# Two preactivated 3x3 convolutions on one Trainium2 core: from 64x64 quarters in two halves to 32x32 blocks in four streams

## What is computed

```python
# x: (8, 16, 512, 512) fp32
def _gn(v, G=8, eps=1e-5):            # group norm over 2 channels x 512 x 512, no weights
    ...
# layer 0: the 3x3 kernel of each image comes from spectral weights, turned by an angle
#          that depends on batch statistics of a 1x1 projection of gn(x)
x = x + _L0_conv_ref(_gn(x), w_fft_real, w_fft_imag, rot_w, rot_b, bn_gamma, bn_beta)
# layer 1: a plain 3x3 convolution with circular padding (written with FFTs)
x = x + _L1_conv_ref(_gn(x), weight)
```

## Time and profile before

| What | us |
|---|---|
| time, median of 2 runs | 1798.58 (1798.43 to 1798.72) |
| profiled execution, time | 1799.18 |
| its span, first to last instruction | 1797.4 |
| PE busy in the span | 1655.8 (92%), 29275 matmuls |
| PE weight loads (PEld) busy | 1246.7 (69%) |
| VectorE busy | 1388.3 (77%) |
| ScalarE busy | 1172.3 (65%) |
| POOL busy | 128.1 (7%) |
| mean DMA rate | 229 GB/s |
| mean granted TensorE clock | 0.977 |

### The profile page before, as it was taken

How to read it: one execution, slowest core, us unless ns; L and a number is a source line. 1 busy time by engine, 2 the same in 40 slices (tenths; PEclk the granted TensorE clock), 3 DMA queues, 4 the chain that set the end, 5 groups by cost and what they waited for, 6 DMA issues and landing times.

```text
span 1797.4 us, 65352 instructions
## 1 busy us (share of the span) xinstructions
PE 1655.8 (92%) x29275; PEld 1246.7 (69%) x29275; DVE 1388.3 (77%) x2175; ACT 1172.3 (65%) x1044; POOL 128.1 (7%) x361
## 2 busy tenths in 40 slices
PE   5887888487779999999999999999999999999899
PEld 5787888333356667887688668866786678666655
DVE  6989999779878787877887888787888788787500
ACT  6888888468556666666666666666666666666444
POOL 0000000120110010002000200020002001100100
PEclk9999999789899999999999999999999999999999
DMA  9999999355446665656666666566656665665245
GB/s 386 421 422 422 422 422 422 146 156 152 126 138 212 206 193 192 218 190 197 207 207 203 188 211 211 198 191 214 202 193 198 206 207 192 202 206 193 96 193 201
DMA packets 101782, 411.56 MB, mean 229 GB/s; under 512 B 16883, under 2 KB 19496, under 8 KB 85160
## 3 DMA queue, kind: packets, MB, share of 16 engines
q1 hardware_dynamic: 100744, 407.81, 64.6%
q0 software_dynamic: 800, 0.15, 0.1%
HBM read 271.82 MB, written 136.07 MB: 227 GB/s over the span
## 4 chain that ended last, share of the span: by engine, by line
PE 72%; DVE 14%; issue 5%; DMA 5%; POOL 1%; ACT 1%; SPq 1%; DVEq 0%; POOLq 0%; ACTq 0%
PE ps L406 36%; PE ps L399 34%; DVE x L635 7%; DMA x<-x_pix 5%; DVE nat L684 2%; DVE x L848 2%; DVE stats L886 1%; ACT x L475 1%; PE ps L350 0%; PE ps L351 0%; SPq L248 0%; PE ps L358 0%; POOL sm L606 0%; DVE ps L854 0%; PE ps L354 0%
## 5 line engine op out<-in xcount | busy, mean ns | idle before, releaser
L399 PE MATMUL ps<-nat,wc 64*64 64x512 f16 (+1 forms) x12480 | 1269.1, 379 | 45.7 <-DVE nat L684 16.5
L406 PE MATMUL ps<-x,wc 64*64 64x512 f16 (+2 forms) x12585 | 1256.4, 375 | 15.3 <-POOL x L615 14.8
L399 PEld LDWEIGHTS ps<-nat,wc 64*64 64x64 f16 x12480 | 721.8, 107 | 252.6 <-issue 38.2
L406 PEld LDWEIGHTS ps<-x,wc 64*64 64x64 f16 x12585 | 732.2, 107 | 193.4 <-POOL x L615 18.5
L500 ACT ACTIVATE nat<-xin,gnp 128x1024 f16<-128x1024 f32 (+1 forms) x264 | 299.9, 1137 | 318.6 <-PE ps L399 306.1
L848 DVE SCALAR_TENSOR_TENSOR x<-ps,gnp,x 128x1024 f16<-128x1024 f32 (+1 forms) x264 | 333.1, 1262 | 28.7 <-ACT x L515 21.5
L530 ACT ACTIVATE outb<-ps,bias 128x1024 f32<-128x1024 f32 (+1 forms) x264 | 289.7, 1097 | 88.5 <-PE ps L406 72.8
L684 DVE SCALAR_TENSOR_TENSOR nat<-xin,gnp,nat 128x1024 f16<-128x1024 f32 (+1 forms) x264 | 332.3, 1259 | 2.0 <-ACT nat L500 1.9
L519 ACT ACTIVATE x<-ps,gnp 128x1024 f16<-128x1024 f32 (+1 forms) x231 | 252.8, 1095 | 107.1 <-DVE stats L886 106.6
L350 PE MATMUL ps<-x 128*128 128x129 f16 x2048 | 258.0, 226 | 59.3 <-DVE x L635 59.2
L635 DVE SCALAR_TENSOR_TENSOR x<-x 128x2048 bf16<-128x2048 f32 x128 | 284.1, 2285 | 17.3 <-ACT x L475 15.6
(11 more groups left out here) (125 smaller groups left out, 273.6 us busy)
## 6 DMA issues: line engine op xcount, KB each, us to landing
x<-x_pix SPq DMA_DIRECT2D x128, 1024.0 KB, 13.5
xin<-x_tiles SPq DMA_DIRECT2D x256, 512.0 KB, 3.8
out<-outb SPq DMA_DIRECT2D x256, 512.0 KB, 4.1
xin<-x_tiles SPq DMA_DIRECT2D x8, 192.5 KB, 2.4
out<-outb SPq DMA_DIRECT2D x8, 192.5 KB, 3.7
w<-taps_scratch SPq DMA_DIRECT2D x64, 8.0 KB, 1.8
w<-taps_scratch SPq DMA_DIRECT2D x28, 16.0 KB, 2.7
taps_scratch<-x POOLq DMA_DIRECT2D x21, 3.0 KB, 3.4
```

Of the source, the lines that this page charges most:

```text
L399: return nc.tensor.matmul(ps[64 * kind:64 * kind + 64, bank, 0:w], lhs, nat[rows, xhl, a:a + w], start=first, stop=last)
L406: ins = nc.tensor.matmul(ps[64 * kind:64 * kind + 64, bank, done:done + part], lhs, x1[rows, xhl, z:z + part], start=first and done == 0, ...
```

## The change

The 64x64 quarter matmuls become 32x32 ones. A group is one of the four input rows (half, r), 32 partitions. Of its four possible output blocks, `outputs` keeps the three that a 3x3 kernel reaches; the fourth holds only zeros and is left out. So each pass of a bank has 12 matmuls, and a bank 72. The four groups are four streams on the same banks, each TRAIL = 7 passes behind the one ahead, and the semaphores `group_done` guard each hand-over. `pe_done` comes with the last block of group 3. Three empty turns (None) per image are put into the list of banks: one behind the last chunk of layer 0, two before the first job of layer 1. On VectorE, image 0 now has `lo0(g + NX)` and then `lo1(g)`; the order for later images stays as it was.

```diff
-TRAIL = 2
+TRAIL = 7
...
-            def quarter(layer, i, n, job, k, half, kind, q, first, last):
+            def outputs(layer, group):
+
+                half, r = divmod(group, 2)
+                found = []
+                for kind in range(2):
+                    row = 2 * (half if kind == 0 else 1 - half) + (r if layer == 0 else 1 - r)
+                    found += [(kind, a) for a in range(2) if 0 <= row - (1 - a if layer == 0 else a) < 3]
+                return found
...
+            def sixteenth(layer, i, n, job, k, group, to, q, first, last):
 
                 whl, xhl, dj = PASSES[k]
-                rows = slice(64 * half, 64 * half + 64)
+                half, (kind, a_) = group // 2, to
+                rows = slice(32 * group, 32 * group + 32)
+                outs = slice(64 * kind + 32 * a_, 64 * kind + 32 * a_ + 32)
...
-                lhs = (wc0 if layer == 0 else wc1)[rows, (i // NCH) % 2, whl, kind, dj, :]
+                lhs = (wc0 if layer == 0 else wc1)[rows, (i // NCH) % 2, whl, kind, dj, 32 * a_:32 * a_ + 32]
...
             banks = [(job, q) for job in range(len(JOBS)) for q in range(banks_of(chunk_of(job)))]
+            for b in range(B):
+                banks.insert(banks.index((JOB0[b * NCH + NFULL], 0)) + 1, None)
+                for _ in range(2):
+                    banks.insert(banks.index((JOB1[b * NCH], 0)), None)
...
-                if at_ >= TRAIL:
-                    pe.wait_ge(lower_done, at_ - TRAIL + 1)
...
+            for at_ in range(len(banks) * len(PASSES) + 3 * TRAIL):
+                for group in range(4):
+                    turn, k = divmod(at_ - group * TRAIL, len(PASSES))
+                    if not 0 <= turn < len(banks):
+                        continue
+                    if banks[turn] is None:
+                        continue
+                    job, q = banks[turn]
+                    layer, i = JOBS[job]
+                    if group == 0 and k == 0:
+                        if q == 0:
+                            ready(job)
...
+                    if group > 0 and k == 0:
+                        pe.wait_ge(group_done[group - 1], turn + 1 - banks[:turn].count(None))
+                    for to in outputs(layer, group):
+                        done = sixteenth(layer, i, chunk_of(job), job, k, group, to, q,
+                                         k == 0 and group == first_group[layer][to], group == last_group[layer][to] and k == len(PASSES) - 1)
+                    if k == len(PASSES) - 1:
+                        if group < 3:
+                            done.then_inc(group_done[group], 1)
+                        elif q == banks_of(chunk_of(job)) - 1:
                             done.then_inc(pe_done, 1)
...
                 elif b == 0:
 
-                    if n > 0:
-                        lo1(g - 1)
                     lo0(g + NX)
-                    if n == NFULL - 1:
-                        lo1(g)
+                    lo1(g)
```

More of the change, by code:

```diff
@@ L204, in conv_program @@
         w0_ready = sem("w0_ready")
-        lower_done = sem("lower_done")
+        group_done = [sem(f"group_done{s}") for s in range(3)]
         pe_done = sem("pe_done")
@@ L386, in _ @@
             mm(ps[:, 7, 16:24], c("ones", C), zc[0:C, 368:376])
[L389 removed]
+            def outputs(layer, group):
[5 more added lines that the diff above has]
+                return found
+            first_group = [{to: min(s for s in range(4) if to in outputs(layer, s))
+                            for to in itertools.product(range(2), range(2))} for layer in range(2)]
+            last_group = [{to: max(s for s in range(4) if to in outputs(layer, s)) for to in first_group[layer]}
+                          for layer in range(2)]
+            def sixteenth(layer, i, n, job, k, group, to, q, first, last):
                 whl, xhl, dj = PASSES[k]
[L392 removed]
+                half, (kind, a_) = group // 2, to
+                rows = slice(32 * group, 32 * group + 32)
+                outs = slice(64 * kind + 32 * a_, 64 * kind + 32 * a_ + 32)
                 w = min(BANK, reads(n) - q * BANK)
@@ L395, in quarter @@
                 bank = CB * (job % SLOTS) + q
-                lhs = (wc0 if layer == 0 else wc1)[rows, (i // NCH) % 2, whl, kind, dj, :]
+                lhs = (wc0 if layer == 0 else wc1)[rows, (i // NCH) % 2, whl, kind, dj, 32 * a_:32 * a_ + 32]
                 if layer == 0:
                     a = (i % NX) * CH + off
-                    return nc.tensor.matmul(ps[64 * kind:64 * kind + 64, bank, 0:w], lhs, nat[rows, xhl, a:a + w],
+                    return nc.tensor.matmul(ps[outs, bank, 0:w], lhs, nat[rows, xhl, a:a + w],
                                             start=first, stop=last)
@@ L405, in quarter @@
                     part = min(w - done, RCOLS - z)
-                    ins = nc.tensor.matmul(ps[64 * kind:64 * kind + 64, bank, done:done + part], lhs,
+                    ins = nc.tensor.matmul(ps[outs, bank, done:done + part], lhs,
                                            x1[rows, xhl, z:z + part], start=first and done == 0, stop=last and done + part == w)
@@ new lines, in _ @@
+            for at_ in range(len(banks) * len(PASSES) + 3 * TRAIL):
[10 more added lines that the diff above has]
+                            ready(job)
+                        if q == banks_of(chunk_of(job)) - 1 and job in means:
+                            b = means[job]
+                            pe.wait_ge(st_in, b + 1)
+                            nc.tensor.matmul(ps[:, CB * ((job - 3) % SLOTS) + 1, 0:2], c("gm"), sm[:, 8:10],
+                                             start=True, stop=True).then_inc(st_pe, 1)
+                    if group > 0 and k == 0:
[7 more added lines that the diff above has]
+                        elif q == banks_of(chunk_of(job)) - 1:
```

1 line of the change is left out of this document (added).

## The result

| | us |
|---|---|
| before, median of 2 (1798.43 to 1798.72) | 1798.58 |
| after, median of 2 (2798.87 to 2803.18) | 2801.02 |
| ratio | 1.557 (1.551 to 1.564) |
| span of the profiled execution, before and after | 1797.4 and 2801.4 |

The change makes the kernel slower by more than half. It adds 1002 us, three times the 311 that were forecast. The stage windows say where. They stand here for after, with the borders that answer to the earlier trace rows: the first convolution matmuls, the first matmul of layer 1, and the last chunk of layer 0 (columns as there).

A forecast was written before the change was run, and what follows sets the result against it. PE bounds the kernel before; afterwards the PSUM slot's return through VectorE would. Span 1797.4 + 3.9 + 43.8 + 2.0 + 256.2 + 5.2 = 2108.5 us, with 1.8 around it 2110 us; range 2040 to 2240, 8 in 10.

The forecast's parts named there:

- Code grows threefold: Instruction fetch: packets rise to 40% of one DMA engine, hidden unless fetching has a latency no row shows; priced 0.
- Some 3 ns each: PE's issue: about 47 instructions after a released weight load, some 3 ns each, support for a step staying 0.217 us.
- longer steps: Rival, chance 0.15: twelve streams don't run side by side, or issue or fetch limits PE; 2191 to 2492 us.
- The blocks: PE's 32x32 matmuls, 72 a bank: a turn stays six steps of 0.217 us; price 0, gain 0.
- The loop: Long stage: PSUM slot's return through PE's longer tail and VectorE sets 6.30 us a chunk pair, +256.2 us; chance 0.69.
- the first stage: Layer 0 alone: a chunk takes 4.9 us instead of 3.53, over 32 chunks +43.8 us.
- The order of VectorE in image 0: First stage: lo1's new place behind lo0 costs nothing more, ending 4.7 us after its mask, just in time.
- lo0 ahead of lo1: VectorE, later images: lo0, 1.27 us, still runs before lo1, so VectorE's 4.03 us becomes part of the slot's return.
- the clock rival: First stage, chance 0.04: clock falls with PE less busy, +1.9 us for each chunk hit; all 32 give 2170 us.
- The last stage: Layer 1 alone: PE binds; a longer tail and waits between groups over 65 turns add 5.2 us.
- The group wait: PE's hand-over between groups on a bank: just fits, 0 to 0.07 us for each of three waits a turn, taken 0.05.
- the empty turns: PE's 24 empty turns lie inside waits on VectorE in the long stage: 0, upper end 31 us.

The follow-up runs named there:

- bench: Kernel before plus six stretches of PE work on standing data behind its last output, in loops or written out; 12 blocks: 0.227 us a step looped, 0.344 written out.
- thirds: Kernel before with each quarter matmul cut in three by columns, 72 matmuls a bank, tiles and order unchanged; 2748.35 us against 1799.99.
- lag21: Changed kernel with its new PE order, empty turns and VectorE order, but 64x64 quarters in two groups, the upper half 21 steps behind; 2135.63 us.
- order_b0: Kernel before with only VectorE's new order in image 0, lo1 of a chunk right behind lo0; 1814.96 us against 1799.11, ratio 1.0087.
- lag12: Changed kernel with 64x64 quarters in two groups, the upper half 12 steps behind as before, empty turns and VectorE's new order kept; 1812.66 us.
- halves: Kernel before with each quarter matmul cut in two by columns, 256 columns each, 48 matmuls a bank; 2108.26 us.

## Why the prediction was wrong

**Where it failed: the fetching of code.** The step is the last one of the stages: "Code grows threefold", which is "40% of one" DMA engine, and then "hidden unless fetching has a latency that no row shows". It was priced at 0 and is the whole of the miss. The share was right as a share: 593 packets are 1.4% of 16 engines, 22% of one. But a share says nothing of a stream in which one packet comes after the other. What counted was the interval, 3.65 us for a block of code with idle DMA queues and 4.05 with the kernel's DMAs, against the 2.3 us in which PE ran it. The rows of before held a bound that I did not work out: 43600 instructions / 256 in 1200.8 us is a block in 7.05 us. Nothing showed that it could be had in 2.3.

**"Some 3 ns each".** As a rate of issue that was sound: 5.2 ns an instruction in the loop of `bench`, 12 blocks in 0.227 us, even 16 in 0.240. It was read within code that was there already, and says nothing of how code arrives. The rival "longer steps" named issue and fetch as possible causes and had 0.15, but its price came from sixteen small matmuls in one place, at most 0.32 us a step. The mean step of the long stage is 4.05 x 12 / 128 = 0.380. The upper end of that unknown was too low, and the range with it. The steps did not get longer, though: 0.215 us each with gaps between them, and the 29 ns of the earlier trace rows do not hold across places.

**The blocks**, "The price is 0": right for streaming, wrong for the number of instructions. By `thirds`, instructions alone take 948 us.

**The loop** was right and was hidden. `lag21` shows 6.30 us for a pair at the place named, 6.38 over an image; the total 2135.6 us stands against 2108.5 + 1.8. Of the 25 us between them the first stage has 208.0 - 191.1 = 17, which the rows put down to the clock (see the first stage below).

**The order of VectorE in image 0**, "costs nothing more": `order_b0` puts it at 15.8 us, but at a lag of 12, where a chunk takes 3.53 us and now (505.2 - 375.2) / 32 = 4.06. The working was for a lag of 21, where a chunk takes 4.9 and lo1, 4.7 us behind its mask, is just in time. No run has the old order at 21 steps. The chunks of `lag21` that ran at the full clock do bear the working out: the 14 of them with a granted clock of 0.97 or more take 4.77 us on average, no longer than forecast.

**lo0 ahead of lo1** was said to be why VectorE "has become half of a loop". The 4.03 us were right as a sum, the reason was not: the chain through ScalarE's line 541 ends 0.04 us before line 870 starts, with lo0 ahead of it or not.

**The first stage** of after took 214.0 us, 6 more than `lag21`. PE's waits there are on lo0, as forecast; the supply needs 1.125 x 4.05 = 4.6 us a chunk, and 5.7 were taken. The granted clock was 0.80 in both for 0.94 before: the clock rival, which had 0.04, came in. Two chunks of `lag21`, one behind the other, show it (windows from one start of line 870 to the next):

```profile
428.21:434.94 6.73, 5.32 (x64) 2.28 (x68) 2.81 (x4) 3.34 (x5) 0.00 (x0) 0.75 0.30 85
434.94:439.71 4.77, 2.79 (x52) 1.28 (x48) 3.26 (x7) 3.34 (x5) 0.00 (x0) 0.97 0.37 110
```

In the timeline PE's 48 matmuls of a chunk take 4.47 us in the first and 2.79 in the second, after idle times of 2.15 and 1.35 us. The chunk is 1.96 us longer, where the rival had 1.9. Over the 32 chunks of `lag21`, 18 have a clock under 0.97 and average 6.05 us, 14 average 4.77; 18 x (6.05 - 4.77) = 23 us covers the 17. That is read from rows; no run parts the clock from the order at this lag. In after it is 21 chunks at 6.27 and 11 at 4.72. Three more slowed chunks make about 4 of the 6 us; the rest stays open.

**The last stage**, +5.2: measured +70.7. PE was to bind, with 128 / 12 x 0.217 us for each block of code; at 39.1 of them 164.4 us are 4.2 each, the tail of the last stores in it. Supply again.

**The group wait**, 0.05 a loop, and **the empty turns**, 0 to 31: neither is seen. Steps run on 0.22 us apart, and `lag12` with its empty turns takes no longer than `order_b0` without.

**Rivals.** PE keeps its order (`lag21` 2135.6, not 1935). Steps do not get short: twelve 32x32 blocks in the loop of `bench` took 0.227 us a step, quarters 0.216. The clock came in, and its 1.9 us for a slowed chunk fit the one shown.

## What to carry to other kernels

Before work is cut into smaller instructions, divide: instructions of the engine per us, written out, over 256, and compare with one block of code in 3.65 us (4.05 beside 120 GB/s of data). Where PE needed one in 3.5 us (`halves`) it cost time, where it needed one in 6.9 nothing. A hot nest that must have so many small matmuls is a case for a hardware loop, like those of 432 and 576 instructions in `bench`, and a lag between streams that share an accumulator is to be kept as short as its hand-over allows, since each step of it comes back in the slot's return.

## What the runs showed of the hardware

- Code written out reaches TensorE at one block of 256 instructions in 3.64 to 3.70 us when little else moves, 4.03 to 4.05 beside 120 GB/s, whether the matmuls have 32 or 512 columns (the idle-queue figures). A loop of 432 or 576 instructions ran without those gaps once its code had come: one instruction packet in 78 us.
- In a loop, TensorE took 24 instructions in 0.124 us, 5.2 ns each, at a granted clock of 0.55. The Trainium skill ("TensorE: Matmul & The Clock Gate", "Wait — 56ns, not 53.3ns?") puts matmul starts no closer than about 25 ns. Blocks in different places do not keep to it here: their matmuls were 10 ns apart.
- The granted clock of the first stage was 0.94 before, where PE waited 23 us on lo0 in all, and 0.80 in `lag21` and after, where it waited 65. A chunk's 48 matmuls then took 4.47 us in a slowed chunk, 2.79 at the full clock.
- Twelve 32x32 places ran 512 columns side by side in 0.227 us a step, sixteen in 0.240, and four 64x64 in 0.216.
